# Decoder layer on one core: expert weights split earlier on GpSimd, routing shared with GpSimd, two early root pairs

## What is computed

```python
x = layernorm(x + self_attention(x))        # 16 heads of 8, learned relative positions, masked beyond 99
x = layernorm(x + cross_attention(x, ctx))  # 16 heads of 8, causal mask
# mixture of experts, 64 experts of width 64:
scores = sigmoid(x @ router_w.T)
sfc    = scores + correction_bias           # 8 groups of 8; a group's score is the sum of its top 2
masked = sfc kept in the best 4 groups, else 0
tidx   = top 8 of masked
tw     = 2.5 * scores[tidx] / (sum + 1e-20)
y      = sum_e combine[:, e] * (relu(x @ up_e)**2 @ down_e) + relu(x @ shared_up)**2 @ shared_down
out    = layernorm(x + y)
```

## Time and profile before

| | us |
|---|---|
| median of 3 runs (lowest, highest) | 279.58 (279.50, 280.51) |
| the profiled execution, its own time | 279.9 |
| its span, first to last instruction | 278.1 |
| PE busy | 254.1 (91%) |
| ACT busy | 215.5 (77%) |
| DVE busy | 202.9 (73%) |
| POOL busy | 142.0 (51%) |

### The profile page before, as it was taken

The page is one execution under the profiler, slowest core; times in us unless marked ns, Lnnn a source line. Parts: engine busy times, 40 slices in busy tenths (PEclk is TensorE's granted clock), DMA queues, the critical chain, the costliest instruction groups (busy, mean ns, idle before and its releaser), DMA issues.

```text
span 278.1 us, 5979 instructions
## 1 busy us (share of the span) xinstructions
PE 254.1 (91%) x1912; PEld 202.5 (73%) x1912; DVE 202.9 (73%) x563; ACT 215.5 (77%) x572; POOL 142.0 (51%) x137
## 2 busy tenths in 40 slices
PE   4989999999999999998896769999998999999991
PEld 3679998788888877776664445668886888788860
DVE  2698736778888889997999973588995457844424
ACT  8572661889999989999998776688897887698861
POOL 5018002400111159654654004488998998699982
PEclk9999999999999999999999988999999999999997
DMA  6719320597623316756660002976581698497201
GB/s 129 179 41 409 102 60 2 142 248 250 176 81 87 97 49 133 181 164 181 171 182 1 1 2 61 244 187 171 179 223 37 166 241 199 142 231 195 78 0 38
DMA packets 52259, 37.94 MB, mean 136 GB/s; under 512 B 15810, under 2 KB 43140, under 8 KB 52228
## 3 DMA queue, kind: packets, MB, share of 16 engines
q1 hardware_dynamic: 52228, 37.57, 50.8%
HBM read 30.48 MB, written 7.08 MB: 135 GB/s over the span
## 4 chain that ended last, share of the span: by engine, by line
PE 58%; DVE 13%; POOL 9%; issue 7%; SPq 5%; DMA 4%; ACT 3%; DVEq 0%; POOLq 0%; ACTq 0%
PE bank L741 20%; PE bank L723 10%; POOL unit_lo L644 6%; PE bank L758 5%; PE bank L776 5%; PE bank L786 4%; PE bank L764 3%; SPq L461 3%; DVE neg_max L1245 3%; PE bank L672 2%; DMA qc_dram<-q_lo 2%; SPq L457 2%; PE bank L679 1%; PE bank L803 1%; DVE scaled L1376 1%
## 5 line engine op out<-in xcount | busy, mean ns | idle before, releaser
L644 POOL TENSOR_TENSOR unit_lo<-unit,unit_hi 128x512 fp32r<-128x512 f32 x68 | 86.5, 1298 | 32.9 <-ACT unit_hi L1093 31.9
L1001 ACT ACTIVATE probs<-bank,neg_max 128x128 f32<-128x128 f32 x224 | 63.9, 395 | 4.5 <-DVE neg_max L1245 4.3
L1376 DVE SCALAR_TENSOR_TENSOR scaled<-bank,roots 128x512 f32<-128x512 f32 x64 | 43.8, 686 | 27.6 <-PE bank L741 22.8
L1092 ACT ACTIVATE unit<-scaled 128x512 f32<-128x512 f32 x68 | 42.9, 630 | 17.2 <-DVE scaled L1376 15.5
L1245 DVE TENSOR_REDUCE neg_max<-bank 128x4 f32<-128x512 f32 x56 | 38.3, 685 | 10.9 <-PE bank L764 10.3
L1093 ACT ACTIVATE unit_hi<-scaled 128x512 fp32r<-128x512 f32 x68 | 42.0, 617 | 0.0
L776 PE MATMUL bank<-ident,probs 128*128 128x128 f32 x256 | 39.0, 275 | 3.1 <-ACT probs L1001 3.1
L776 PEld LDWEIGHTS bank<-ident,probs 128*128 128x128 f32 x256 | 30.1, 140 | 8.5 <-ACT probs L1001 5.4
L764 PE MATMUL bank<-k_bd,q_stk 128*128 128x512 f32 x64 | 34.0, 532 | 0.0
L723 PE MATMUL bank<-spread,rel_t 128*128 128x128 f32 x256 | 28.9, 275 | 0.0
L723 PEld LDWEIGHTS bank<-spread,rel_t 128*128 128x128 f32 x256 | 28.7, 192 | 0.1
(11 more groups left out here) (212 smaller groups left out, 479.4 us busy)
## 6 DMA issues: line engine op xcount, KB each, us to landing
roots<-root_dram SPq DMA_DIRECT2D x60, 256.0 KB, 4.7
q_stk<-q_dram SPq DMA_DIRECT2D x16, 128.0 KB, 3.0
k_bd<-k_dram SPq DMA_DIRECT2D x32, 64.0 KB, 2.3
incoming<-in_L_ffn_up_w SPq DMA_DIRECT2D x4, 512.0 KB, 4.6
q_stk<-qc_dram SPq DMA_DIRECT2D x16, 128.0 KB, 3.1
k_bd<-kc_dram SPq DMA_DIRECT2D x32, 64.0 KB, 2.5
incoming<-in_L_ffn_down_w SPq DMA_DIRECT2D x4, 512.0 KB, 4.5
k_dram<-k_hi SPq DMA_DIRECT2D x2, 512.0 KB, 3.4
```

Source lines behind the costliest of these rows:

```text
L644: nc.gpsimd.tensor_tensor(unit_lo[:, k % R], unit[:, k % 3], unit_hi[:, k % R], ALU.subtract).then_inc(lo_ready, 1)
L1001: last = nc.scalar.activation(probs[:, U % 3, h4 * L:(h4 + 1) * L], ps[BS[U % 3]][:, h4 * L:(h4 + 1) * L], ACT.Exp, bias=neg_max[:, U % 4, ...
L1092: nc.scalar.activation(unit[:, k % 3], scaled[:, k % 3], ACT.Square)
L1376: ins = nc.vector.scalar_tensor_tensor(scaled[:, k % 3], h, 0.0, roots[:, n % ROOT_RING, c % ROOTS], ALU.max, ALU.mult)
```

## The change

1. The tiles `w_hi` and `w_lo` become one tile `w_parts`, whose eight blocks lie each where the 16 heads' positions of one sequence lie. `pos` is therefore ordered by sequence and then head. POOL splits piece B in its loop at B = 0 to 7, once the scores of sequence B are done. SP loads piece B-2 at B = 4 to 9.
2. In the routing of batches 0 and 1 eight operations go from DVE to POOL (add one, add the bias, mask, weight, combine and three for the root), and DVE gets one small one. Each change of engine is a semaphore. POOL's order is: tokens' low parts of sequences 0 and 1, its share of batch 0, low parts of 2 and 3, its share of batch 1, and then the `unit_lo`.
3. Batch 0 runs at 1.9 parts per step: it ends at step 58 in place of 61. `first_roots(0)` moves with it. Batch 1 keeps its steps.
4. `EARLY` is 2: two pairs are spread by PE and ACT, and the loads of roots begin with the set of pairs 2 and 3.
5. `weights_out` stands before `queries_out` in ACT's step, and takes the factor 0.5 of the first half's roots.

```diff
-EARLY = 2 * ROOTS
+EARLY = ROOTS
-BATCHES = [(range(0, 2), 1.35), (range(2, 4), 2.7), (range(4, 6), 1.4), (range(6, 8), 1.4)]
+BATCHES = [(range(0, 2), 1.9), (range(2, 4), 2.7), (range(4, 6), 1.4), (range(6, 8), 1.4)]
...
-                if 2 <= B - 7 < NB:
-                    load_piece(B - 7)
+                if 2 <= B - 2 < NB:
+                    load_piece(B - 2)
...
-                if B >= NB:
-                    b = B - NB
-                    if b == 0:
-                        pool.wait_ge(ld["sup"], 16)
-                        pool.wait_ge(ld["sdn"], 16)
-                        pool.wait_ge(scores_ready, NU)
-                        pool.wait_ge(kc_kept, 16 * REPS)
...
+                if B < NB:
+
+                    pool.wait_ge(ld[f"piece{B % 2}"], 16 * (B // 2 + 1))
+                    pool.wait_ge(scores_ready, NG * (B + 1))
+                    nc.gpsimd.tensor_copy(w_parts[:, B, 0], incoming[:, B % 2]).then_inc(w_high, 1)
+                    pool.wait_ge(w_high, B + 1)
+                    nc.gpsimd.tensor_tensor(w_parts[:, B, 1], incoming[:, B % 2], w_parts[:, B, 0],
                                             ALU.subtract).then_inc(w_split, 1)
...
+            def route_share(q):
...
+                pool.wait_ge(logit_exp, seqs[-1] + 1)
+                pool.wait_ge(ld["corr"], 16)
+                nc.gpsimd.tensor_scalar(r_one[:, at, :], r_exp[:, at, :], 1.0, None, ALU.add).then_inc(one_made, 1)
+                pool.wait_ge(sig_made, q + 1)
+                nc.gpsimd.tensor_tensor(biased[:, at, :], score[:, at, :],
+                                        corr_row[:, :].unsqueeze(1).broadcast_to([128, size, E]), ALU.add)\
+                    .then_inc(biased_made, 1)
+                pool.wait_ge(keep_made, q + 1)
...
+                pool.wait_ge(chosen_made, q + 1)
...
+                pool.wait_ge(wrec_made, q + 1)
...
+                pool.wait_ge(root_newton, q + 1)
+                link(nc.gpsimd.tensor_tensor(root_sum[:, at, :], comb[:, at, :], inverse, ALU.mult))
+                link(nc.gpsimd.tensor_tensor(inverse, root_sum[:, at, :], base, ALU.add))
+                nc.gpsimd.tensor_tensor(root[:, at, :], inverse, chosen[:, at, :], ALU.mult).then_inc(root_made, 1)
+
+            for q in range(2):
+                for b in BATCHES[q][0]:
+                    tokens_low(b)
+                route_share(q)
...
-                pe.wait_ge(root_ready, 2 * (f + 1))
+                pe.wait_ge((root_made, root_ready)[f], 2)
...
+                if part == 1 and shared_out:
+                    dve.wait_ge(one_made, q + 1)
+                    nc.vector.reciprocal(sig, one).then_inc(sig_made, 1)
...
                 if part == 10:
+                    if shared_out:
+                        dve.wait_ge(masked_made, q + 1)
...
+                    if shared_out:
+                        dve.wait_ge(weight_made, q + 1)
```

More of the change, by code:

```diff
@@ L116, in piece, with expert_weights @@
     return n // (NB // 2), slice(n % (NB // 2) * size, (n % (NB // 2) + 1) * size)
+def expert_weights(w_parts, way, c):
+    per_piece = 2 * NPAIR // NB
+    cols = slice(c % per_piece * 128, (c % per_piece + 1) * 128)
+    return [w_parts[:, way * NB // 2 + c // per_piece, part, cols] for part in range(2)]
 def h_bank(k):
@@ L631, in _ @@
-            for k in range(-1, 2 * CH):
-                if k in (-1, REST2):
-                    for b in range(0 if k < 0 else HB, HB if k < 0 else NB):
-                        cols = slice(b * L, (b + 1) * L)
-                        pool.wait_ge(xt_out, NB + b + 1)
-                        nc.gpsimd.tensor_tensor(x2_lo[:, cols], x2_t[:, cols], x2_hi[:, cols],
-                                                ALU.subtract).then_inc(x2_split, 1)
[L639 to L643, removed]
-                    nc.gpsimd.tensor_tensor(unit_lo[:, k % R], unit[:, k % 3], unit_hi[:, k % R],
-                                            ALU.subtract).then_inc(lo_ready, 1)
+                if B == 0:
+                    pool.wait_ge(ld["sup"], 16)
+                    pool.wait_ge(ld["sdn"], 16)
+                    nc.gpsimd.tensor_copy(sh_hi[:, :, :], shared[:, :, :]).then_inc(shared_high, 1)
+                    pool.wait_ge(shared_high, 1)
+                    nc.gpsimd.tensor_tensor(sh_lo[:, :, :], shared[:, :, :], sh_hi[:, :, :], ALU.subtract)
@@ new lines, in _ @@
+            for q in range(2):
+                for b in BATCHES[q][0]:
+                    tokens_low(b)
+                route_share(q)
+            for k in range(2 * CH):
+                if k == REST2:
+                    for b in range(HB, NB):
+                        tokens_low(b)
+                pool.wait_ge(hi_ready, k + 1)
+                if k >= R:
+                    pool.wait_ge(down_done, k - R + 1)
+                nc.gpsimd.tensor_tensor(unit_lo[:, k % R], unit[:, k % 3], unit_hi[:, k % R],
+                                        ALU.subtract).then_inc(lo_ready, 1)
@@ L860, in expert_up @@
                 if c >= 0:
-                    w = [t[:, 0, c * 128:(c + 1) * 128] for t in (w_hi, w_lo)]
+                    w = expert_weights(w_parts, 0, c)
                 else:
@@ L1109, in _ @@
                     tokens_out(at_step(s, TOKENS))
+                if s - 1 in CT:
+                    weights_out(CT.index(s - 1))
                 if at_step(s, USE) is not None:
@@ L1352, in route @@
                     last.then_inc(comb_ready, 1)
-                if part == 14:
+                if part == 14 and not shared_out:
                     base, inverse = first_root_tiles(q)
```

99 lines of the change are left out of this document (68 added, 31 removed).

## The result

| | before | after |
|---|---|---|
| median (lowest, highest), runs on one chip | 280.04 us (279.50, 281.52), 4 runs | 287.09 us (285.17, 289.57), 4 runs |
| ratio, 95% interval | | 1.0212 (1.0167 to 1.0257) |
| profiled execution, its own time | 279.9 us | 285.17 us |
| its span | 278.1 us | 283.3 us |

The changed kernel is 2.1% slower, about 6 us. The direction was forecast; the time, 281.3 us with a range up to 284.3, was not. The profiled execution of after is the shortest of its four and shows 5.2 us of the difference in its span.

A forecast was written before the change was run, and what follows sets the result against it. PE was taken to bound the experts, DVE the stretch from 150 to 165 us, with SP's queue close behind; +3.7 loop, +0.5 routing, -2.1 pairs, -0.3 gap gave +1.8, so 281.3 us, range 277.0 to 284.3.

The forecast's parts named there:

- loop: Weight loads, splits and query stores over SP, POOL and DMA: 10.0 us per turn against 6.5 of attention, delaying unit 44; +3.7 us.
- routing: Routing of batches 0 and 1 shared with POOL: DVE time freed becomes a wait, handovers cancel savings; turn_weights(0) +0.5 us.
- pairs: Two spread root pairs fewer on PE, which is the limit behind turn_weights(0): -2.1 us.
- a shorter gap: On ACT, one stall of DVE behind POOL disappears, taking 0.3 us back.
- Where the loop starts: Piece 2 issued at 67.70, then two loads of 0.45 and gathers of 4.84 us, so piece 4 at 78.3.
- The side cost: Two POOL subtractions meet layer norms in the self attention; priced at nothing, up to 1.3 us net without unit 44's wait.
- The sign that was named for the loop: In the changed trace PE should idle 3 to 5 us before unit 44, ending with keys landing.
- the queue named in the forecast: On POOL, batch 1's addition of one stands behind batch 0's root operations and low parts; unit 60's maxima wait, +0.4 us.
- C: Rival: long gaps idle PE, clock stays low over spread roots and first up products; +4 to +5, 284 us; chance 0.14.
- A: Rival: the loop over SP, POOL and DMA doesn't bind; about -2.9, 276.7 us; chance 0.15.
- B: Rival: the loop binds but half as much, +1.5; 279.5 us, no difference; chance 0.18.
- D: Rival: routing gain comes in full (-3, POOL in time for batch 1) with the loop binding; -1, 278.5 us; chance 0.13.

The follow-up runs named there:

- e9_normonly: Changed kernel with one edit: POOL's split of piece B (2 and more) also waits for the layer norm of sequence B-1; 287.5 us, ratio 1.0256.
- e8_hit: e7_phase with POOL's splits waiting for one more unit of scores and no norm, so subtractions fall under layer norms; 280.75 and 285.2 us, two runs.
- e7_phase: Changed kernel with splits right behind norms, loads a turn earlier, query split behind piece b+2, batch 1's addition of one ahead; 276.91 us, ratio 0.9812.
- e1_loop: Changed kernel with POOL splitting queries of sequence b ahead of piece b+4 and SP loading pieces ahead of query stores; 282.0 us, ratio 1.0008.
- e2_chop: Changed kernel with POOL's subtraction of each weight piece cut into four of 256 columns, queue orders kept; 290.23 us, ratio 1.0364.
- e3_both: Changed kernel with the edits of e1_loop and e2_chop together; 280.24 us, ratio 1.0003.
- e6_route: e3_both with the routing of batches 0 and 1 on DVE alone, batch 0 at 1.35 parts per step again; 279.6 us, ratio 0.9954.
- e5_first: e3_both with POOL's addition of one for batch 1 ahead of its three root operations for batch 0; 280.69 us, ratio 0.9949.
- e4_early: Kernel before with one edit, two early spread root pairs (EARLY = ROOTS); 279.25 us, ratio 0.9941.
- e10_all: e7_phase with four early spread root pairs again (EARLY = 2 * ROOTS); 279.63 us, ratio 0.9953.

## Why the prediction was wrong

The sum was +3.7 (loop) +0.5 (routing) -2.1 (pairs) -0.3 (a shorter gap) = +1.8. In the profiled spans the terms came out as +7.0, -0.3 and -2.9, and the preparation's spread of +1.4: together +5.2. Point by point:

- **The loop: right mechanism, mis-sized term.** This is the step that failed: +3.7 us was forecast for the loop, +7.0 measured, 3.3 more. The forecast chain was unit 44 at 125.2, then 6.3 us for four units and 1.3 to the exponentials of unit 48, 132.8. Less the 1.4 of unit 0, after has unit 44 at 127.5, 135.44 - 128.86 = 6.6 us for four units, and the exponentials at 137.41, 2.0 behind their scores. So 2.3 us come from the loop's place, 0.3 from the pace, and 0.7 from the assumption that ACT's backlog would empty: the 2.0 us between scores and exponentials, taken for backlog, are the same in a starved pipeline. On ACT's timeline of after:

```profile
137.41 1.15 ACT L1056 ACTIVATE probs<-bank,neg_max 128x128 f32<-128x128 f32 x4
```

- **Where the loop starts.** Two gathers at "up to 4.84 us with DMA busy" were assumed between pieces 2 and 4. The one beside the load of piece 2 took 77.74 - 70.30 = 7.4 us; its two query loads were issued in 3.83 us, where the same two took 2.15 in the earlier trace rows. Nor was 4.84 the longest of the trace of before: the gather at 61.12 there took 5.4. Piece 4 was issued at 83.08, or 81.7 less unit 0, and not at 78.3: +3.4. The turns themselves, taken as 10.0, were 9.5 on the mean, which gave 1.6 back, and from the store of sequence 3 to unit 44 it took 8.3 us where 8.0 were counted. The range was also reckoned wrong: the chain from piece 4 to the store holds four landings, so the shortest ones would have made it 2.8 us shorter and not 2.1. That is at the low end and did not decide the miss.
- **The side cost, priced at nothing because "unit 44's wait swallows it".** In the changed kernel this was right (e9_normonly: half a microsecond). Its size without that wait was not: "up to 1.3 net" from two meetings, where after has four, 5.3 us of norms, of which PE waited 0.67 + 1.69 + 0.32 + 2.52 = 5.2, and e8_hit against e7_phase priced such stalls at nearly their full length. The count failed because it asked only when a split may start by the scores; the pieces came late by the loop, at any phase of the attention, and POOL's casts hold DVE too. It moved the time of this kernel by no more than the runs can tell, but it set that of e8_hit. The sign that was named for the loop, PE idle for 3 to 5 us before unit 44, was not seen (1.25): the stalls had made PE late before the keys were. With fewer stalls it came nearer: 2.58 us at unit 44 in e9_normonly, behind 1.93 at unit 40.
- **The two causes don't add.** Against after, taking away the loop gains 5.0 us at turn_weights(0) (e1_loop), taking away a part of the stalls, 2.2 and 3.7 us of PE's waits, gains nothing (e9_normonly, e2_chop), and taking away both gains 5.6 (e3_both).
- **Routing.** The idle time of DVE ahead of batch 1's reciprocal was forecast as 2 to 3 us and is 1.96; from the maxima of unit 60, now at 159.66, to turn_weights(0) 13.75 us were forecast and 172.99 - 159.66 = 13.3 measured. DVE's timeline of after, with its two waits for handovers, and then PE's:

```profile
158.79 0.95 DVE L1354 RECIPROCAL score<-r_one 128x128 f32<-128x128 f32 x1 [1.96 <-POOL r_one L662]
159.66 0.63 DVE L1300 TENSOR_REDUCE neg_max<-bank 128x4 f32<-128x512 f32 x1
...
166.69 0.35 DVE L1397 MAX8 etop<-masked 128x8 f32<-128x64 f32 x2 [0.58 <-POOL masked L669]
...
169.00 0.28 DVE L1415 TENSOR_REDUCE wsum<-weight 128x2 f32<-128x128 f32 x1 [0.65 <-POOL weight L674]
```

```profile
172.99 0.62 PE L898 MATMUL bank<-ident,root 128*64 128x128 f32 x4 [1.54 <-POOL root L685]
```

  From unit 48 to turn_weights(0) after is 0.3 us shorter than before (+6.96 to +6.65); in the kernels whose attention was nearly on time the sharing cost 1.3 (e6_route against e3_both), somewhat more than the 0.5 forecast, and the queue named in the forecast is the cause (e5_first).
- **The early pairs.** -2.1 forecast, -1.7 measured on its own (e4_early, and in e10_all with the low clock beside it). After has 1.1 us more than that in its experts. The windows of after show the granted clock low from 161 to 164, ahead of turn_weights(0), behind the gap of PE at 160; the kernel before had it behind, at 166, where PE works on the experts. e3_both, e4_early, e6_route and e7_phase have it there too, and their experts take 111.4 to 111.7 us. That it makes up the 1.1 us fits, but was not tested.

```profile
160.00:161.00 1.00, 0.17 (x1) 0.14 (x1) 0.97 (x5) 0.68 (x3) 0.28 (x1) 0.99 0.00 0
161.00:162.00 1.00, 1.00 (x6) 0.92 (x6) 0.93 (x13) 1.00 (x5) 0.00 (x0) 0.50 0.00 0
162.00:163.00 1.00, 1.00 (x4) 0.71 (x4) 1.00 (x7) 0.58 (x3) 0.00 (x0) 0.50 0.00 0
163.00:164.00 1.00, 1.00 (x6) 0.94 (x5) 0.87 (x8) 1.00 (x5) 0.00 (x0) 0.50 0.03 8
```

- **Rivals.** C ("worse than forecast", 284 us) came nearest in time but not by its mechanism: the clock was not low over the spread roots, where C wanted it. It did fall behind the stall at 110, and cost PE about 1.1 us there (3.67 - 2.52), which the wait for keys at unit 44 then swallowed. A and B are refuted by e1_loop and e9_normonly (the loop binds in full), D, for the routing as the change has it, by e6_route.
- **What stays open.** The ratio of 1.0212 is 5.9 us, while the two spans differ by 5.2, of which the 1.4 of unit 0 is no effect of the change. So some 2 us of the difference lie in executions that no trace shows; the mean granted clock of the three others was 0.971 to 0.973, of the traced one 0.983. Why the two query loads beside piece 2 took 3.83 us to issue is open too. And a place in one trace carries an error: unit 44 moved by 1.3 us in e4_early with nothing changed ahead of it, so terms of a few tenths of a us are no more than bookkeeping.

## What to carry to other kernels

When work moves to another place in two in-order queues, write the loop through both queues out with the slowest gather the trace can give, and give what feeds the next stage (here the queries) priority over what is only prefetched. e1_loop, which does just this, turned +2.1% into +0.1%; e7_phase, which also keeps POOL's splits off the norms and mends the order at the routing, into -1.9%. Before GpSimd gets long instructions beside VectorE's latency-critical ones, ask in which phase each will fall, and tie their start to the instruction that they must not meet. Undoing one of two overlapping causes may show nothing (e9_normonly), so undo both, and each.

## What the runs showed of the hardware

- A layer norm on DVE (tensor_scalar, 128x128 fp32, SBUF to SBUF) that meets a POOL instruction under way ends behind it, be it a subtraction (2.36 us) or a cast (1.04 us): 0.34 us became up to 2.50, with 0.07 to 0.08 us from the end of the one to that of the other in the four meetings of after and the four of e8_hit. Where the norm began first (117.20 in after) it took its 0.34, and the subtraction 2.45.
- POOL's subtraction of 128x1024 took 2.34 to 2.38 us whole and 2.80 us in four parts: the cut costs 0.44.
- The six DMAs of the gather behind the load of piece 2 were issued over 7.4 us, those of the others in that stretch over 4.2 to 5.9 us. The time stands in the issuing instructions' own durations (3.83 us for two, 3.57 for four). The load alone doesn't make it: two of the shorter gathers (4.6 and 4.2 us) stood behind such a load too.
- Behind PE's wait of 2.52 us at 110 in after the granted clock was at 0.50 until about 113, and four transpositions took 1.06 us in place of 0.60.
